# VectorE takes the first probability addition of each attention unit, GpSimd all later ones

## The reference

```python
x = _layernorm(x + attn(x, w_qkv))            # x: (8, 1024, 512) float32, 16 heads of 32
x = _layernorm(x + ffn(x, w_gate, w_up, w_down))
# attn:
scores = jnp.einsum('bnqd,bnkd->bnqk', q, k) / jnp.sqrt(jnp.float32(h))
probs = jax.nn.softmax(scores, axis=-1)
ctx = jnp.einsum('bnqk,bnkd->bnqd', probs, v)
# ffn: all operands quantised and dequantised to FP4 in blocks of 16
```

## Time and profile before

| | |
|---|---|
| median of 3 runs | 3920.85 us (3920.46 to 3924.07) |
| the profiled execution | 3922.93 us, its span 3921.3 us |
| PE busy | 3744.5 us, 95% |
| DVE busy | 3024.0 us, 77% |
| POOL busy | 2232.0 us, 57% |
| ACT busy | 1709.7 us, 44% |
| mean granted PE clock over the span | 0.988 of full speed |

### The profile page before, as it was taken

How to read it: one execution, slowest core, us unless ns; L and a number is a source line. 1 busy time by engine, 2 the same in 40 slices (tenths; PEclk the granted TensorE clock), 3 DMA queues, 4 the chain that set the end, 5 groups by cost and what they waited for, 6 DMA issues and landing times. The chain is left out here.

```text
span 3921.3 us, 61535 instructions
## 1 busy us (share of the span) xinstructions
PE 3744.5 (95%) x22853; PEld 1727.3 (44%) x22853; DVE 3024.0 (77%) x5075; ACT 1709.7 (44%) x3085; POOL 2232.0 (57%) x1427
## 2 busy tenths in 40 slices
PE   3599999999999999999999999999999999999999
PEld 2244454344544355443544445434454334544354
DVE  9876787678876688667877678767887668866787
ACT  2166423663246532555226542366424553255522
POOL 1298624984268832787229862398425883278722
PEclk9699999999999999999999999999999999999999
DMA  5211101011011110111101110101101111010110
GB/s 169 81 36 34 55 21 37 17 43 48 25 31 32 35 47 20 43 27 35 47 20 39 31 57 20 39 17 42 49 22 33 30 37 46 20 42 25 31 52 22
DMA packets 106565, 152.53 MB, mean 39 GB/s; under 512 B 28176, under 2 KB 55568, under 8 KB 106128
## 3 DMA queue, kind: packets, MB, share of 16 engines
q1 hardware_dynamic: 106256, 148.49, 12.2%
HBM read 76.28 MB, written 19.66 MB: 24 GB/s over the span
## 5 line engine op out<-in xcount | busy, mean ns | idle before, releaser
L604 DVE TENSOR_REDUCE mx<-R 128x1 f32<-128x512 f32 x2080 | 1316.9, 683 | 536.1 <-PE R L698 533.1
L1265 ACT ACTIVATE arena<-SC 128x512 f32<-128x512 f32 x1360 | 755.6, 603 | 407.9 <-PE SC L1531 279.2
L1606 PE MATMUL SC<-wgu,split 128*128 128x512 f16 (+1 forms) x3456 | 714.5, 361 | 0.0
L1176 POOL TENSOR_TENSOR arena<-arena,sc_h 128x704 f32<-128x704 bf16 (+1 forms) x144 | 178.0, 1250 | 606.1 <-DVE arena L528 606.1
L1150 POOL TENSOR_TENSOR wd<-wd,arena 128x1024 f32<-128x1024 f32 x212 | 494.2, 2358 | 44.5 <-ACT arena L1265 44.5
L1606 PEld LDWEIGHTS SC<-wgu,split 128*128 128x128 f16 x3456 | 338.3, 98 | 331.4
L1265 ACT ACTIVATE wd<-SC 128x512 f32<-128x512 f32 x688 | 389.8, 603 | 211.8 <-PE SC L1531 149.1
L1307 ACT ACTIVATE arena<-SC,gain 128x512 f32<-128x512 f32 (+1 forms) x192 | 125.1, 651 | 810.2 <-PE R L1606 411.9
L678 PE MATMUL R<-xT,wqkv 128*128 128x512 bf16 x1632 | 421.5, 380 | 19.5 <-DVE xT L591 13.1
L698 PE MATMUL R<-ks_even,qs_even 96*128 96x512 bf16 x1056 | 395.0, 389 | 27.6 <-DVE mx L604 7.8
L698 PE MATMUL R<-arena 96*128 96x512 bf16 x1024 | 374.0, 382 | 13.2 <-DVE xT L591 8.2
(11 more groups left out here) (138 smaller groups left out, 5496.6 us busy)
## 6 DMA issues: line engine op xcount, KB each, us to landing
x<-n_L_attn_embeddings_dram SPq DMA_DIRECT2D x136, 256.0 KB, 2.8
wd<-wd_kept SPq DMA_DIRECT2D x32, 512.0 KB, 5.4
out_dram<-x SPq DMA_DIRECT2D x64, 256.0 KB, 2.0
ks_even<-split SPq DMA_DIRECT2D x204, 64.0 KB, 2.0
qs_even<-split SPq DMA_DIRECT2D x408, 32.0 KB, 1.8
arena<-split SPq DMA_DIRECT2D x192, 64.0 KB, 2.0
arena<-split SPq DMA_DIRECT2D x384, 32.0 KB, 1.8
wd<-wd_kept SPq DMA_DIRECT2D x16, 384.0 KB, 7.2
```

Source lines behind the costliest of these rows:

```text
L604: nc.vector.reduce_max(mx[:, j:j + 1], ring_of(ring, job)[:, :], AX_X).then_inc(max_done, 1)
L1176: nc.gpsimd.tensor_tensor(blocks_of(q_h[:, cols]), blocks_of(r_h[:, cols]), spread(sc_h[:, c], c.stop - c.start), ALU.mult).then_inc(qh_do ...
L1265: nc.scalar.activation(probs_of(s)[:, hd, :], SC[e % SLOTS][:, :], ACT.Exp, scale=SCALE).then_inc(exp_done, 1)
L1606: last = nc.tensor.matmul(GU[kk % 2][which][:, 0:w], xhT[i % 2][:, part_x * KH + k, :], wgu[:, part_w * KH + k, which * I + first:which * ...
```

## The change

The first addition of every unit (tiles 0 and 1) moves from GpSimd to DVE, as two additions of 128x1024 in step 2 of the unit, after DVE's second maximum of that step. GpSimd starts with tile 2 and adds one tile more than before: up to tile 7 (tile 5 in the last unit). So the "sum" job on PE takes only the accumulator (in the last unit the accumulator and tiles 6 and 7).

```diff
-POOL_SUMS = [TILES - 2] * (UNITS - 1) + [TILES // 2]
+POOL_SUMS = [TILES - 1] * (UNITS - 1) + [TILES // 2 + 1]
+FIRST_SUM_STEP, FIRST_SUM_MAX = 2, 2
...
+        first_sum = sem("first_sum")
...
-            return 2 * (sum(pool_sums(v) for v in range(u)) + t - 1) + i + 1
+            return 2 * (sum(pool_sums(v) - 1 for v in range(u)) + t - 2) + i + 1
...
                     def sum_probs(u, t, i):
                         s, hs = TILES * u + t, slice(2 * i, 2 * i + 2)
                         pool.wait_ge(exp_done, GROUP * s + 2 * i + 2)
-                        if t == 1:
-                            if u >= 2:
-                                pool.wait_ge(ring_full, ring.full(("sum", u - 2, 0)))
-                            if u >= UNITS and u % UNITS == 0:
-                                for par in range(2):
-                                    pool.wait_ge(stored[par], 16 * TILES // 2 * (u // UNITS))
-                            first = probs_of(s - 1)[:, hs, :]
+                        if t == 2:
+                            pool.wait_ge(first_sum, 2 * u + i + 1)
                         else:
                             pool.wait_ge(pool_sum, sums_done(u, t - 1, i))
-                            first = acc[u % 2][i]
-                        nc.gpsimd.tensor_tensor(acc[u % 2][i], first, probs_of(s)[:, hs, :], ALU.add).then_inc(pool_sum, 1)
+                        nc.gpsimd.tensor_tensor(acc[u % 2][i], acc[u % 2][i], probs_of(s)[:, hs, :], ALU.add).then_inc(pool_sum, 1)
...
-                            for t in range(1, pool_sums(u) + 1):
-                                if ends and t == pool_sums(u):
+                            for t in range(2, pool_sums(u) + 1):
+                                if ends and t == pool_sums(u) - 1:
                                     inverse_deviation("x", TILES * b)
...
-                        if t <= pool_sums(u):
-                            act.wait_ge(pool_sum, sums_done(u, max(t, 1), i))
+                        if t < 2:
+                            act.wait_ge(first_sum, 2 * u + i + 1)
+                        elif t <= pool_sums(u):
+                            act.wait_ge(pool_sum, sums_done(u, t, i))
                         else:
                             act.wait_ge(ring_full, ring.full(("sum", u, 0)))
...
+                    def first_sums(u):
+                        s = TILES * u
+                        if u >= 2:
+                            dve.wait_ge(ring_full, ring.full(("sum", u - 2, 0)))
+                        if u >= UNITS and u % UNITS == 0:
+                            dve.wait_ge(qx_done, TILES * (u // UNITS))
+                            for par in range(2):
+                                dve.wait_ge(stored[par], 16 * TILES // 2 * (u // UNITS))
+                        for i in range(2):
+                            hs = slice(2 * i, 2 * i + 2)
+                            dve.wait_ge(exp_done, GROUP * (s + 1) + 2 * i + 2)
+                            nc.vector.tensor_tensor(acc[u % 2][i], probs_of(s)[:, hs, :], probs_of(s + 1)[:, hs, :],
+                                                    ALU.add).then_inc(first_sum, 1)
...
+                            n_max = 0
                             for kind, a, j in jobs:
...
                                 elif kind == "max":
                                     maximum(a, j)
+                                    n_max += 1
+                                    if t == FIRST_SUM_STEP and n_max == FIRST_SUM_MAX:
+                                        first_sums(u)
```

## The result

The changed kernel takes 3938.5 us (median of 7 runs, 3934.28 to 3941.27), the one before 3923.82 (7 runs, 3920.46 to 3925.25): ratio 1.0038, 95% interval 1.0027 to 1.0050. The forecast was 3943. The profiled execution has a span of 3936.8 us, 15.5 more than before.

A forecast was written before the change was run, and what follows sets the result against it. PE's order of work bounds the kernel, GpSimd next. Per batch 6.9 us saved, 3.3 lost at unit 1, 0.85 at unit 3, 5.5 at the end: +22 us over eight batches, forecast 3943 us (own range 3929 to 3961; overall 3903 to 3966).

The forecast's parts named there:

- PE's saving: In "sum" of every unit PE does one group of products less: 0.86 us each, 55 us over 64 units.
- DVE's additions: Two additions, 2.45 us a unit, cost nothing in units 1 to 7; in unit 0 DVE is 1.07 us late, nothing added.
- Exclusion and unit 0: GpSimd cannot run beside DVE's additions in unit 0, so PE waits 3.3 us before "sum" in unit 1.
- S(1): Moment PE comes to "sum" in step 2 of unit 1 (likewise for other units); its start forecast 3.3 us later.
- How the shift runs on: After unit 1's wait, PE waits 0.85 us before "sum" in unit 3, and not in units 2 and 4 to 7.
- The end of the stage: Attention's end: GpSimd's fifth tile delays the last "sum" and `quantise_x`; `gate_up` comes 3.75 us later relative to unit 7's "sum".
- GpSimd's next addition goes ahead of a waiting DVE: In `quantise_x`, a waiting DVE operation gets through only when GpSimd's tile 5 ends, at 458.4 instead of 453.85.
- A: GpSimd and DVE do not exclude each other in these additions and `quantise_x`: -14 us, 3907 us; chance 0.20.
- B: All waits are hidden and the 0.86 us saved in "sum" counts every time: 3866 us; chance 0.06.
- C: Units as forecast, but `quantise_x` slips between GpSimd's additions or PE's queue absorbs it; end costs +1.4: 3924 us; chance 0.16.
- D: DVE becomes late in each unit, PE's maxima wait for banks, five units lose their 0.86: 3978 us; chance 0.09.
- The sum: Per batch -1.0 up to "sum" of unit 7 and +3.75 at the end: +2.75 us, times 8 +22 us.

The follow-up runs named there:

- e4_dve_alone: Changed kernel, but GpSimd stops at its old last tile (6, in the last unit 4), so "sum" is as long as before; DVE still makes the first addition: 3927.68 us.
- e2_last: Changed kernel, but in the last unit GpSimd adds only up to tile 4 and PE takes tiles 5, 6 and 7: 3918.46 us, ratio 0.9986.
- e5_dummy_last: Against e2_last, GpSimd makes two more additions after tile 4 in the last unit, whose result nobody takes: 3926.06 us, ratio 1.0011 to the kernel before.

## Why the prediction was right

**PE's saving.** Right: "sum" of one group runs 0.86 us, the stretches S3-S4, S4-S5 and S5-S6 are 6.7 to 8.2 us shorter over eight batches (8 x 0.86 = 6.9).

**DVE's additions.** Right in units 1 to 7, taken as nothing; e4_dve_alone and the changed kernel's own stretches show it. In unit 0 I added nothing because PE would wait for GpSimd longer anyway. That holds for the changed kernel, but the 1.07 us of lateness is real: 0.7 to 0.9 a batch, seen as soon as GpSimd's wait is gone.

**Exclusion and unit 0.** Right. The start of "sum" at S(1) was forecast 3.3 us later a batch, and it is 3.3 (26.5 / 8). It is not all wait: PE stands 1.9 to 2.3 us before it, at or under the lower end of the 2.3 to 3.3 that were to show it, and comes 1.2 us later itself, of which DVE's uncovered additions make 0.9 (e4_dve_alone). The forecast's order (DVE both additions, then GpSimd) is not quite what happens: GpSimd's first is issued after DVE's first and waits inside, with the same end. The Trainium skill, "SBUF — State Buffer", section "SBUF: two separate sides", has the two block each other for a whole instruction, whichever starts first. The trace agrees: 3.18 and 3.21 us for GpSimd's first additions, 2.48 us for DVE's. (Of the rows that the prediction named for it, only the earlier trace rows has a DVE operation with two inputs; those of the earlier trace rows have one, and were held back all the same.)

**How the shift runs on.** S(3): forecast wait 0.85, measured 0.62 in the first batch. (The 1.24 us taken for `add` is 1.28 in the earlier trace rows; the 29.1 us it goes into stay.) S1-S2 failed in size. It should be 0.86 shorter than before. It is so in four batches; in the four others it is 0.8, 0.8, 0.3 and 0.8 longer. There PE's clock falls to its lower level behind the wait:

```profile
698.75 0.62 PE L712 MATMUL R<-x,ones 128*32 128x512 f32 x2 [2.08 <-POOL spill L1146]
...
699.60 1.75 PE L1563 MATMUL CT<-wd,v_even 128*32 128x512 f32 x8
701.06 2.01 PE L1563 MATMUL CT<-arena,v_even 128*32 128x512 f32 x8
```
```profile
690.00:697.50 7.50, 6.30 (x30) 2.14 (x26) 6.14 (x11) 5.92 (x11) 7.50 (x4) 1.00 0.01 2
697.60:704.00 6.40, 5.25 (x29) 1.47 (x30) 3.68 (x3) 0.84 (x2) 4.21 (x2) 0.73 0.00 0
```

The second fence is the view by stretch (columns as in the earlier trace rows). The granted clock is 1.00 before and 0.73 in the stretch of `weigh`, whose eight products take 1.75 and 2.01 us instead of 1.04. That is 1.1 to 1.7 us a time, 6 us in all, which the working had not priced. In the other four batches PE idled as long (2.31 us in the first) and its clock stayed. The lower level is 1.2 of 2.4 GHz.

At S6-S7 the opposite luck: -11.7 instead of -6.9. The kernel before had lost 2.4 us in each of two batches:

```profile
1351.87 0.38 PE L698 MATMUL R<-ks_even,qs_even 96*128 96x512 bf16 x1 [1.09 <-DMA qs_even<-split]
...
1353.21 1.94 PE L1546 MATMUL CT<-arena 128*32 128x512 f32 x8
```
```profile
1352.00:1357.00 5.00, 5.00 (x32) 1.52 (x31) 1.38 (x2) 0.30 (x1) 2.47 (x2) 0.66 0.17 47
```

(Both of the kernel before.) A wait of 1.09 us for a copy and a clock of 0.66 behind it; in the changed kernel neither occurs. The two errors, +6 and -5, cancel.

**The end of the stage.** Right in its place and its kind, too large by 0.7 us a batch: S(7) to `gate_up` was forecast as 32.9, it is 32.2 (29.2 before). The forecast let the transpose follow `scale_x`; what it follows is the first maximum behind `quantise_x`, which ends 0.26 us after `scale_x`. Two more statements of that step failed. The timeline of the changed kernel, DVE and POOL:

```profile
450.45 0.21 DVE L514 TENSOR_SCALAR sc_x<-amax 128x32 f32<-128x32 f32 x1
...
451.08 1.89 DVE L516 TENSOR_SCALAR inv<-inv 128x32 f32<-128x32 f32 x1
...
452.87 4.68 POOL L1146 TENSOR_TENSOR wd<-wd,arena 128x1024 f32<-128x1024 f32 x2
453.00 2.29 DVE L518 TENSOR_SCALAR sc_x<-sc_x 128x32 f32<-128x32 f32 x1
...
455.33 2.77 DVE L524 TENSOR_TENSOR split<-x,inv 128x512 f32<-128x512 f32 x1
...
460.43 1.06 POOL L1162 TENSOR_TENSOR split<-spill,sc_x 128x512 f32<-128x512 bf16 x1 [2.88 <-DVE spill L530]
...
461.09 1.25 DVE L606 TENSOR_REDUCE mx<-R 128x1 f32<-128x512 f32 x2
```

"GpSimd's next addition goes ahead of a waiting DVE" is not so here. At each end of one of GpSimd's additions DVE got one operation through: L516 ended at 452.97, L518 at 455.29, L524 at 458.10. None lasted 5 us. So `quantise_x` was two operations further than I took when GpSimd ended (457.55), and `scale_x` started 0.6 us earlier relative to S(7) (28.1 against 28.7). The case of the earlier trace rows on which I had built it (914.81) does not bear the rule. There a DVE operation begins 0.07 us before the recorded end of one addition and sits through the whole next one. The same operation of the kernel before begins 0.06 to 0.07 us before that end in seven batches; in two (914.81, 2782.04) it takes 2.42 us, in the other five 0.18. In the changed kernel it is one batch of seven:

```profile
917.56 2.41 DVE L514 TENSOR_SCALAR sc_x<-amax 128x32 f32<-128x32 f32 x1
```

So close to the boundary it goes either way, and the kernel before already showed it. Those that had waited through most of an addition always got in.

The other statement: I let PE come to the last "sum" 0.86 earlier relative to S(7) and then wait 3.0 us. It waits 2.17 us, since it was already stopped at 447.49: GpSimd's `add` ends, relative to S(7), only 0.2 us before where it ended before, DVE idles 0.82 us for it (0.19 before), and its maxima free PE's bank late, 1.48 us of wait (0.85 before). So 0.6 of the 0.86 us was gone there, whether or not the last unit adds a fifth tile, which is also 5 of the 11 us by which e2_last stayed above its expectation. The start of "sum" came out right (25.3 us after S(7), forecast 25.4), its two waits divided otherwise.

**The rivals.** A (no exclusion) is refuted by the lengths 3.2 and 2.48 us. B would need no wait at S(1) and none at the end. C was right that DVE's operations slip through between the additions, one at a time; but the end costs 3.0 us, not its 1.4. D is refuted by e4_dve_alone for the long "sum" and by the changed kernel's stretches from S(3) to S(6) for the short one.

**The sum.** Forecast +22 in the profiled execution, measured +15.5: the end 5.6 less, S6-S7 4.8 less, S1-S2 6 more, and the rest is about 2 less. That the total came out this close is in part luck, since what the clock did at S1-S2 and S6-S7 was in no term and cancelled.

## What to carry to other kernels

When work moves from the engine that bounds the kernel to one that is half idle by its mean, price it where that engine has no gap: here two places a batch (the unit without slack, and the end of the stage, where another engine's short operations had to wait for its additions) lost more than the sixty-four groups of products saved, and giving the bounding engine those two groups back turned +0.4% into -0.3%. Look then at what starts the busy engine's chain: the same additions placed one maximum earlier gave another 0.2%, two maxima later cost 6%. Look last at what is queued behind the delayed chain: PE's wait for the fifth tile, the one in plain sight, was covered by a longer one for a bank that the delayed engine held. A short wait of TensorE can cost twice: the wait, and the products behind it at the lower clock.

## What the runs showed of the hardware

- Exclusion between GpSimd and DVE holds for small operations too: DVE's TENSOR_SCALAR on 128x32 takes 0.18 us alone and 1.89 and 2.29 us beside GpSimd's additions. GpSimd's own addition takes 3.2 us instead of 2.36 when DVE's second addition is under way.
- At the boundary between two GpSimd additions a DVE operation that has waited through most of the addition gets in, one for each boundary: three times in a row at the end of the changed kernel's first batch, and as often in the other batches. One that begins 0.06 to 0.08 us before the boundary goes either way: 0.18 us in five of seven batches of the kernel before and in six of seven of the changed kernel, 2.4 us in the others. In e5_dummy_last, where GpSimd's two dummies follow each other with a gap of 0.08 us, two got in there (L518 and the next).
- After a wait of 1.9 to 2.3 us at S(1) PE's clock fell to its lower level in four of eight batches (the second, fourth, sixth and eighth) and stayed up in the others. In e2_last it fell at the same place in the second, third, fourth and sixth, in e5_dummy_last in the first and eighth. I could not tell the two apart by the length of the wait or the place.
